# Cross-attention on one core: the ragged memory tile summed in four products, its lower-half terms laid behind the upper ones

## The chip, the core and the metric

The kernel runs on one core of a Trainium2 chip. The metric is the device time of one execution in microseconds. Five engines work side by side, each with an instruction queue of its own: TensorE (PE, products and transposes), VectorE (DVE), ScalarE (ACT), GpSimd (POOL) and SyncE (SP, which here only waits and issues transfers). They meet through semaphores, which are counters that one engine raises and another waits for. A transfer (DMA) raises its semaphore by 16 once it has landed.

## The reference, cut to what matters

Eight batches; in each, 512 rows of `x` with 512 features attend to M = 1601 rows of memory with 256 features.

```python
memory_proj = einsum('bme,de->bmd', memory, W_mem)            # (8, 1601, 512)
scores = einsum('bnd,bmd->bnm', hidden_states, memory_proj) / sqrt(512)
attn = softmax(scores, axis=-1)                                # over the 1601 memory rows
memory_context = einsum('bnm,bmd->bnd', attn, memory_proj)
gate_input = concatenate([hidden_states, memory_context], axis=-1)
gate = sigmoid(einsum('bnf,df->bnd', gate_input, W_gate) + b_gate)
fused = hidden_states + gate * memory_context
return rmsnorm(fused, norm_w)
```

Inputs and output are float32.

## The kernel before, in words

The kernel never forms `memory_proj`. It turns x into q = W_memᵀ xᵀ (256 x 512 per batch), takes scores against the raw memory, sums the memory rows with the softmax weights (u, 256 x 512), and applies W_mem to u behind that.

**Precision by halves.** Every operand of a product stands as two `float32r` tensors, an upper half (`_hi`, written by ScalarE as a rounded copy) and a lower half (`_lo`, the rest, written by VectorE as the difference of the original and the copy). A product of two such operands is three products: hi·hi, hi·lo and lo·hi.

**Tiles.** The 1601 memory rows make MT = 13 tiles of 128 partitions; the last (t = 12) has LAST = 65 rows. A batch on TensorE is, in this order: `scores` (13 tiles x 2 halves of the features x 3 products), the gate and context products of the batch before, `gate_x`, and then `weighted(b, t)` for t = 0 to 12, which sums memory rows times softmax weights over the partitions: for each of the two halves c of the memory's features L529 multiplies `mem_hi` by `p_hi`, L530 `mem_hi` by `p_lo`, L531 `mem_lo` by `p_hi`, six products of 512 columns a tile, for the last tile with 65 rows each. They add up in `bank0` (c = 0) and `bank1` (c = 1). Behind t = QUERY_AT = 9 stand the 24 products of `query`, which make the q of the next batch. Behind t = 12 the scores of the next batch follow at once.

**Softmax.** For each tile VectorE subtracts the maximum (`shift`), ScalarE takes the exponential into `p_tmp` and its rounded copy into `p_hi` (L640), and VectorE writes `p_lo` (L848, a ring of ten tiles), which raises `p_has_lo`. TensorE waits for `p_has_lo` before each tile of `weighted`. `p_hi` lies in the same memory as the scores `s`. In batch 0 ScalarE's queue has both `q_hi_part`s of the next batch ahead of the last `p_hi_part`; in the batches behind it they stand behind the loop over the tiles.

**Memory rows.** SyncE loads memory rows into `mem_raw`, two tiles a pair (L259) and the last tile's 65 rows alone (L261); ScalarE (`mem_hi_part`) and VectorE (`mem_lo_part`) split a pair into `mem_hi` and `mem_lo`. Two more sets of loads (`mem_blocks`, `x_raw`) bring memory and x in blocks of 32 for VectorE's transposes.

**SyncE's queue.** One queue issues all of these in program order, and a wait at its head holds everything behind it. An iteration of the loop is: x of the next batch (L241, 16 transfers), its memory blocks (L249), two loads of x again (L270), the rest of this batch's memory rows (L259, L261), memory blocks (L249, L252), x again, the first memory rows of the next batch (L259), and the four stores of the batch before (L275), each behind `out_done`. Batch 0 has a start of its own ahead of the loop, which ends with the loads of batch 1's first memory rows; the last batch stands behind the loop.

Of the kernel before, what the change touches and what calls it, by code (L numbers as in the profile page):

```python
# [36 lines left out]
P = 128  # L37
# [6 lines left out]
def xattn_kernel(nc: bass.Bass, x, mem, w, wg, b_gate, norm_w, out):  # L44
# [9 lines left out]
    LO_RING = 10  # L54
    RAW_PAIRS = 4
    ROW_BLOCKS = -(-M // BLOCK)
    assert N == 512 and D == 512 and C == 256 and MT % 2 == 1 and M % BLOCK == 1

    def rows(t):
# [2 lines left out]
    with ExitStack() as ctx:  # L62

        def sb(name, shape, dt=F32):
            return ctx.enter_context(nc.sbuf_tensor(name, shape, dt))

        def sem(name):
            return ctx.enter_context(nc.semaphore(name))
# [5 lines left out]
        p_tmp = sb("p_tmp", [P, TMP_RING, N])  # L74
        p_lo = sb("p_lo", [P, LO_RING, N], F32R)
        mem_raw = sb("mem_raw", [P, 2 * RAW_PAIRS, C])

        mem_blocks = sb("mem_blocks", [P, CT, ROW_BLOCKS, BLOCK])
        mem_hi = sb("mem_hi", [P, MT, C], F32R)
# [75 lines left out]

        in_x_first = [sem(f"in_x_first{k}") for k in range(NT)]
        in_mem = [sem(f"in_mem{p}") for p in range(MP)]

        in_blocks = [sem(f"in_blocks{g}") for g in range(2)]

# [73 lines left out]
        @block.sync  # L234
        def _(sp):
            def load_x(b):
                for k in range(DT):
                    for a in range(BLOCKS):
                        d = k * P + a * BLOCK
                        src = x[b, :, d : d + BLOCK].rearrange("(r j) i -> j r i", j=BLOCK)  # L240
                        sp.dma_start(x_blocks[a * BLOCK : (a + 1) * BLOCK, k, :, :], src).then_inc(in_x, 16)  # L241

            def load_mem_blocks(b, g):
                r0, r1 = ((0, 4 * P // BLOCK), (4 * P // BLOCK, ROW_BLOCKS - 1))[g]
                for c in range(CT):
                    for a in range(BLOCKS):
                        f = c * P + a * BLOCK
                        src = mem[b, r0 * BLOCK : r1 * BLOCK, f : f + BLOCK].rearrange("(r j) i -> j r i", j=BLOCK)
                        sp.dma_start(mem_blocks[a * BLOCK : (a + 1) * BLOCK, c, r0:r1, :], src).then_inc(in_blocks[g], 16)  # L249
                if g == 1:  # L250

                    sp.dma_start(mem_blocks[0:P:BLOCK, :, r1, :],  # L252
                                 mem[b, M - 1, :].rearrange("(c a i) -> a c i", c=CT, i=BLOCK)).then_inc(in_blocks[g], 16)

            def load_mem(b, p):
                slot = 2 * (p % RAW_PAIRS)
                if p < MP - 1:
                    src = mem[b, 2 * p * P : (2 * p + 2) * P, :].rearrange("(t p) c -> p t c", p=P)
                    sp.dma_start(mem_raw[:, slot : slot + 2, :], src).then_inc(in_mem[p], 16)  # L259
                else:  # L260
                    sp.dma_start(mem_raw[0:LAST, slot, :], mem[b, (MT - 1) * P : M, :]).then_inc(in_mem[p], 16)  # L261

            def load_mem_again(b, p):

                behind = p - RAW_PAIRS if p >= RAW_PAIRS else min(p + RAW_PAIRS, MP - 1) - MP
                sp.wait_ge(mem_has_lo, MP * b + behind + 1)
                load_mem(b, p)

            def load_x_again(b, j):
                sp.dma_start(x_again[:, j % 2, :], x[b, j * P : (j + 1) * P, :]).then_inc(in_x_again[j % 2], 16)  # L270

            def store(b, j):

                sp.wait_ge(out_done, NT * b + j + 1)
                sp.dma_start(out[b, j * P : (j + 1) * P, :], fused[:, j, :]).then_inc(fused_free[j], 16)  # L275

            def iteration(b, last):
                if not last:

                    sp.wait_ge(xt_done, DT * b)  # L280
                    load_x(b + 1)
                    sp.wait_ge(mt_done, MP * b)
                    load_mem_blocks(b + 1, 0)

                load_x_again(b - 1, 0)
                load_x_again(b - 1, 1)
                for p in range(RAW_PAIRS, MP):
                    load_mem_again(b, p)
                if not last:

                    sp.wait_ge(mt_done, MP * b + MP - 2)
                    load_mem_blocks(b + 1, 1)
                for j in range(2, NT):

                    sp.wait_ge(fused_done, NT * (b - 1) + j - 1)
                    load_x_again(b - 1, j)
                if not last:
                    for p in range(RAW_PAIRS):
                        load_mem_again(b + 1, p)
                for j in range(NT):  # L300
                    store(b - 1, j)


            for j in range(NT):
                sp.dma_start(x_raw[:, j, :], x[0, j * P : (j + 1) * P, :]).then_inc(in_x_first[j], 16)
            for p in range(2):
                load_mem(0, p)

            sp.wait_ge(ready_pad, 1)
            load_mem_blocks(0, 1)  # L310
            for p in range(2, RAW_PAIRS):
                load_mem(0, p)
            for i in range(DT):
                sp.dma_start(wg_raw[i], wg[i * P : (i + 1) * P, :]).then_inc(in_wg, 16)
            sp.dma_start(bias_rows[:, :], b_gate.partition_broadcast(P)).then_inc(in_rows, 16)
            sp.dma_start(norm_rows[:, :], norm_w.partition_broadcast(P)).then_inc(in_rows, 16)

            load_mem_blocks(1, 0)
            for p in range(RAW_PAIRS, MP):
                load_mem_again(0, p)  # L320

            sp.wait_ge(mt_done, MP - 2)
            load_mem_blocks(1, 1)

            sp.wait_ge(pe_wt, V[-1] + 1)
            load_x(1)
            for p in range(RAW_PAIRS):
                load_mem_again(1, p)
            with sp.Fori(1, B - 1) as b:
                iteration(b, False)  # L330
            iteration(B - 1, True)

            load_x_again(B - 1, 0)
            load_x_again(B - 1, 1)
            for j in range(2, NT):

                sp.wait_ge(fused_done, NT * (B - 1) + j - 1)
                load_x_again(B - 1, j)
            for j in range(NT):

                if 0 < j < NT - 1:
                    sp.wait_ge(tail_done, j)
                else:
                    sp.wait_ge(out_done, NT * (B - 1) + (1 if j == 0 else 2))
                sp.dma_start(out[B - 1, j * P : (j + 1) * P, :], fused[:, j, :]).then_inc(fused_free[j], 16)

            for j in range(NT):
                sp.wait_ge(fused_free[j], 16 * (B + 1))
# [3 lines left out]
        def _(pe):  # L352
# [143 lines left out]
            def gate_x(b, j, first):  # L496
# [18 lines left out]
                    (xt_hi[:, k, n], xt_lo[:, k, n], wg1t_hi[:, k, :], wg1t_lo[:, k, :]) for k in range(DT)  # L515
                ]).then_inc(pe_gx, 1)

            def weighted(b, t):

                if t % 2 == 0:  # L520

                    pe.wait_ge(mem_has_lo, MP * b + t // 2 + 1)

                pe.wait_ge(p_has_lo, MT * b + t + 1)
                r = rows(t)
                for c in range(CT):
                    cs = slice(c * P, (c + 1) * P)
                    dst = bank[U_BANK + c][:, :]
                    nc.tensor.matmul(dst, mem_hi[0:r, t, cs], p_hi[0:r, t, :], start=(t == 0), stop=False)  # L529
                    nc.tensor.matmul(dst, mem_hi[0:r, t, cs], p_lo[0:r, t % LO_RING, :], start=False, stop=False)  # L530
                    last = nc.tensor.matmul(dst, mem_lo[0:r, t, cs], p_hi[0:r, t, :], start=False, stop=(t == MT - 1))  # L531
                    if c == 0 and t == MT - 1:
                        last.then_inc(pe_u_first, 1)
                last.then_inc(pe_u, 1)
# [31 lines left out]
            def iteration(b, first, last):  # L566
# [31 lines left out]

                    pe.wait_ge(gx_done, NT * b + 2)
                for t in range(MT):  # L600
                    weighted(b, t)
                    if t == QUERY_AT and not last:

                        pe.wait_ge(xt_has_lo, DT * (b + 2))
                        pe.wait_ge(gx_done, NT * (b + 1))
                        for c in range(CT):
                            query(c, range(DT))
# [30 lines left out]
        def _(act):  # L638
            def copy(dst, src):
                return nc.scalar.activation(dst, src, ACT.Copy)  # L640
# [12 lines left out]
            def mem_hi_part(b, p, first):  # L653
                if p == 0 and not first:

                    act.wait_ge(pe_u, MT * b)

                act.wait_ge(in_mem[p], 16 * (b + 1))
                ts, raw, r = mem_pair(p)
                copy(mem_hi[0:r, ts, :], mem_raw[0:r, raw, :]).then_inc(mem_has_hi, 1)  # L660

            def copy_s(b, t):
# [537 lines left out]
```

## Time and profile before

| | |
|---|---|
| Time, three runs | 549.3, 549.71 and 549.73 us; median 549.71 |
| Time of the profiled execution | 550.2 us |
| Its span, first to last instruction | 548.4 us |
| TensorE busy | 535.8 us (98%), 2432 products and transposes |
| VectorE, ScalarE, GpSimd busy | 483.7 us (88%), 335.2 us (61%), 145.5 us (27%) |
| Granted TensorE clock, mean | 0.994 of full |
| DMA, all queues | 54.25 MB, 42% of 16 engines' span |

Busy time of TensorE counts each product from its start to a modelled end, and neighbours overlap; the distance between two starts says what a product costs in a row of them. The chain that ended last follows from the last instruction back to whatever released each step, so that its shares say which engine sets the end. A wait of an engine that is not on that chain costs nothing by itself.

### The profile page before, as it was taken

Reading aid. Unit: us, or ns where it says so; the run is one execution under the profiler, and the core shown is the slowest. Engines: PE = TensorE matmul, PEld = TensorE weight load, DVE = VectorE, ACT = ScalarE, POOL = GpSimd, SP = SyncE. Lnnn points to the kernel's source line nnn. Section 1 sums busy time; section 2 is a strip of 40 time slices with the busy share of each in tenths; the row PEclk is TensorE's granted clock in tenths of the full one; section 3 lists DMA queues with packets and bytes.
Section 4 is the critical chain, followed back from the end, with each engine's and each line's share of the span. In section 5 each row is a group of like instructions: output and inputs, shape, how many; then the busy total and the mean of one; then the engine's idle time right before and its main releaser. Section 6 shows DMA issues by size and latency. Waiting matters only on the chain.

```text
span 548.4 us, 8870 instructions
## 1 busy us (share of the span) xinstructions
PE 535.8 (98%) x2432; PEld 438.6 (80%) x2432; DVE 483.7 (88%) x759; ACT 335.2 (61%) x633; POOL 145.5 (27%) x120
## 2 busy tenths in 40 slices
PE   8999999999999999999999999999999999999993
PEld 7776888888888888888888888888888888888882
DVE  3779968899799998899888997999989999889965
ACT  4576636666476655576466764666656765657544
POOL 0005600165002540036200650025400273005600
PEclk9999999999999999999999999999999999999997
DMA  9865372611585207831278114763068411201033
GB/s 225 258 125 85 93 113 76 107 58 41 125 169 96 79 0 162 183 85 38 77 126 171 57 38 111 162 100 90 5 148 178 105 38 39 95 27 38 1 116 115
DMA packets 184337, 54.25 MB, mean 99 GB/s; under 512 B 161528, under 2 KB 174848, under 8 KB 184320
## 3 DMA queue, kind: packets, MB, share of 16 engines
q1 hardware_dynamic: 183792, 53.52, 42.2%
q10 hardware_dynamic: 528, 0.52, 0.3%
q8 instruction: 8, 0.13, 0.1%
q14 instruction: 9, 0.07, 0.0%
HBM read 45.63 MB, written 8.39 MB: 99 GB/s over the span
## 4 chain that ended last, share of the span: by engine, by line
PE 92%; SPq 3%; DMA 2%; DVE 1%; issue 1%; ACT 0%; POOLq 0%; ACTq 0%; POOL 0%; DVEq 0%
PE bank L357 21%; PE bank L359 21%; PE bank L358 21%; PE bank L529 9%; PE bank L530 9%; PE bank L531 9%; DMA fused<-in_L_xattn_W_gate_dram 2%; SPq L249 2%; PE bank L549 1%; PE bank L459 1%; PE bank L563 1%; PE bank L444 1%; PE bank L432 1%; DVE fused L1001 1%; DVE fused L994 1%
## 5 line engine op out<-in xcount | busy, mean ns | idle before, releaser
L1150 POOL TENSOR_TENSOR psum_rows<-psum_rows,p_tmp 128x512 f32<-128x512 f32 (+1 forms) x88 | 124.1, 1411 | 72.7 <-ACT p_tmp L678 71.2
L848 DVE TENSOR_TENSOR p_lo<-p_tmp,p_hi 128x512 fp32r<-128x512 f32 (+1 forms) x104 | 93.4, 899 | 5.5 <-ACT p_hi L640 5.4
L678 ACT ACTIVATE p_tmp<-s 128x512 f32<-128x512 f32 (+1 forms) x104 | 65.1, 627 | 38.2 <-DVE s L889 37.6
L1150 POOL TENSOR_TENSOR psum_rows<-p_tmp 128x512 f32<-128x512 f32 x8 | 10.8, 1353 | 276.2 <-ACT p_tmp L678 276.2
L357 PE MATMUL bank<-q_hi,mt_hi 128*128 128x512 f32 (+1 forms) x208 | 81.8, 393 | 0.0
L358 PE MATMUL bank<-q_lo,mt_hi 128*128 128x512 f32 (+1 forms) x208 | 81.2, 390 | 0.0
L359 PE MATMUL bank<-q_hi,mt_lo 128*128 128x512 f32 (+1 forms) x208 | 81.2, 390 | 0.0
L530 PE MATMUL bank<-p_lo,mem_hi 128*128 128x512 f32 (+1 forms) x208 | 81.0, 389 | 0.0
L529 PE MATMUL bank<-p_hi,mem_hi 128*128 128x512 f32 (+1 forms) x208 | 81.0, 389 | 0.0
L531 PE MATMUL bank<-p_hi,mem_lo 128*128 128x512 f32 (+1 forms) x208 | 80.9, 389 | 0.0
L640 ACT ACTIVATE s<-bank 128x512 f32<-128x512 f32 (+1 forms) x104 | 62.1, 597 | 19.5 <-PE bank L359 19.1
L889 DVE TENSOR_TENSOR s<-s,bank 128x512 f32<-128x512 f32 (+1 forms) x104 | 68.5, 672 | 0.0
L860 DVE TENSOR_TENSOR run<-run,s 128x512 f32<-128x512 f32 (+1 forms) x88 | 60.0, 681 | 8.1 <-ACT s L640 5.8
L640 ACT ACTIVATE p_hi<-p_tmp 128x512 fp32r<-128x512 f32 (+1 forms) x104 | 63.5, 617 | 0.0
L357 PE MATMUL bank<-wg1t_hi,xt_hi 128*128 128x512 f32 x128 | 50.2, 392 | 0.0
L359 PE MATMUL bank<-wg1t_hi,xt_lo 128*128 128x512 f32 x128 | 49.8, 389 | 0.0
L358 PE MATMUL bank<-wg1t_lo,xt_hi 128*128 128x512 f32 x128 | 49.8, 389 | 0.0
L848 DVE TENSOR_TENSOR mt_lo<-bank,mt_hi 128x512 fp32r<-128x512 f32 (+1 forms) x56 | 34.6, 628 | 16.6 <-ACT mt_hi L640 16.6
L640 ACT ACTIVATE mt_hi<-bank 128x512 fp32r<-128x512 f32 (+1 forms) x56 | 30.1, 550 | 28.9 <-PE bank L359 28.9
L531 PEld LDWEIGHTS bank<-p_hi,mem_lo 128*128 128x128 f32 (+1 forms) x208 | 39.0, 188 | 8.2
L359 PEld LDWEIGHTS bank<-q_hi,mt_lo 128*128 128x128 f32 (+1 forms) x208 | 38.2, 184 | 9.2
L529 PEld LDWEIGHTS bank<-p_hi,mem_hi 128*128 128x128 f32 (+1 forms) x208 | 39.0, 188 | 8.2
(92 smaller groups left out, 1024.5 us busy)
## 6 DMA issues: line engine op xcount, KB each, us to landing
mem_raw<-in_ctx_dram SPq DMA_DIRECT2D x48, 256.0 KB, 3.0
mem_blocks<-in_ctx_dram SPq DMA_DIRECT2D x64, 136.0 KB
x_again<-in_x_dram SPq DMA_DIRECT2D x32, 256.0 KB, 2.7
out_dram<-fused SPq DMA_DIRECT2D x32, 256.0 KB, 2.1
x_raw<-in_x_dram SPq DMA_DIRECT2D x112, 64.0 KB, 2.0
mem_blocks<-in_ctx_dram SPq DMA_DIRECT2D x56, 64.0 KB, 2.0
x_raw<-in_x_dram SPq DMA_DIRECT2D x4, 256.0 KB, 4.9
gate<-in_L_xattn_W_gate_dram SPq DMA_DIRECT2D x2, 512.0 KB, 5.8
```

Source lines behind the costliest of these rows:

```text
L357: nc.tensor.matmul(dst, a_hi, b_hi, start=(start and i == 0), stop=False)
L358: nc.tensor.matmul(dst, a_hi, b_lo, start=False, stop=False)
L359: last = nc.tensor.matmul(dst, a_lo, b_hi, start=False, stop=(stop and i == n - 1))
L529: nc.tensor.matmul(dst, mem_hi[0:r, t, cs], p_hi[0:r, t, :], start=(t == 0), stop=False)
L530: nc.tensor.matmul(dst, mem_hi[0:r, t, cs], p_lo[0:r, t % LO_RING, :], start=False, stop=False)
L531: last = nc.tensor.matmul(dst, mem_lo[0:r, t, cs], p_hi[0:r, t, :], start=False, stop=(t == MT - 1))
L640: return nc.scalar.activation(dst, src, ACT.Copy)
L678: nc.scalar.activation(p_tmp[0:r, t % TMP_RING, :], s[0:r, t, :], ACT.Exp, scale=float(D) ** -0.5).then_inc(exp_done, 1)
L848: return nc.vector.tensor_tensor(dst, src, hi.bitcast(F32), ALU.subtract)
L860: nc.vector.tensor_tensor(run[0:r, :], a, s[0:r, t, :], ALU.max).then_inc(run_done, 1)
L889: nc.vector.tensor_tensor(s[0:r, t, :], s[0:r, t, :], bank[MAX_BANK][0:r, :], ALU.subtract).then_inc(shifted, 1)
L1150: nc.gpsimd.tensor_tensor(psum_rows[0:r, :], a, p_tmp[0:r, t % TMP_RING, :], ALU.add).then_inc(p_added, 1)
```

## The change

For the last tile of a batch (except in the last batch, which stays as it was) the 63 free partitions behind its 65 rows are used. BEHIND is 63, REST is 2.

- `mem_raw` gets a second load for that tile: the tile's first 63 rows again, on partitions 65 to 127. `in_mem[6]` then counts 32 a batch. `mem_hi_part` copies all 128 partitions of it, so that `mem_hi` holds the 65 rows and, behind them, the first 63 again. (`r = P` in it changes nothing for the other pairs.)
- `stack_last_tile(b)` on SyncE makes four transfers inside the on-chip memory: the upper half of the last 2 memory rows to `mem_lo` behind its 65 rows (after `mem_has_lo`), and, after the last `p_has_lo` of the batch, the first 63 rows of `p_lo` to `p_hi` behind its 65 rows, the 65 rows of `p_hi` to a new tile `lo_terms`, and the last 2 rows of `p_lo` behind them. All four raise `stacked`.
- `weighted_last_tile(b)` waits for `stacked` at 64 a batch and multiplies for each c `mem_hi` by `p_hi` over 128 partitions (hi·hi of 65 rows and hi·lo of 63) and `mem_lo` by `lo_terms` over 67 partitions (lo·hi of 65 rows and hi·lo of 2): four products in place of six.
- In SyncE's queue `stack_last_tile` stands between the loads of the next batch's memory rows and the stores; for batch 0 it is the last thing ahead of the loop.

```diff
@@ -54,6 +54,8 @@
     LO_RING = 10
     RAW_PAIRS = 4
     ROW_BLOCKS = -(-M // BLOCK)
+    BEHIND = P - LAST
+    REST = LAST - BEHIND
     assert N == 512 and D == 512 and C == 256 and MT % 2 == 1 and M % BLOCK == 1
 
     def rows(t):
@@ -74,6 +76,8 @@
         p_tmp = sb("p_tmp", [P, TMP_RING, N])
         p_lo = sb("p_lo", [P, LO_RING, N], F32R)
         mem_raw = sb("mem_raw", [P, 2 * RAW_PAIRS, C])
+
+        lo_terms = sb("lo_terms", [P, N], F32R)
 
         mem_blocks = sb("mem_blocks", [P, CT, ROW_BLOCKS, BLOCK])
         mem_hi = sb("mem_hi", [P, MT, C], F32R)
@@ -156,6 +160,8 @@
         in_x_first = [sem(f"in_x_first{k}") for k in range(NT)]
         in_mem = [sem(f"in_mem{p}") for p in range(MP)]
 
+        stacked = sem("stacked")
+
         in_blocks = [sem(f"in_blocks{g}") for g in range(2)]
 
         in_x_again = [sem(f"in_x_again{i}") for i in range(2)]
@@ -259,6 +265,22 @@
                     sp.dma_start(mem_raw[:, slot : slot + 2, :], src).then_inc(in_mem[p], 16)
                 else:
                     sp.dma_start(mem_raw[0:LAST, slot, :], mem[b, (MT - 1) * P : M, :]).then_inc(in_mem[p], 16)
+                    sp.dma_start(mem_raw[LAST:P, slot, :], mem[b, (MT - 1) * P : (MT - 1) * P + BEHIND, :]
+                                 ).then_inc(in_mem[p], 16)
+
+            def stack_last_tile(b):
+                def copy(dst, src):
+                    sp.dma_start(dst.bitcast(F32), src.bitcast(F32)).then_inc(stacked, 16)
+
+                t, behind = MT - 1, slice(LAST, LAST + REST)
+
+                sp.wait_ge(mem_has_lo, MP * (b + 1))
+                copy(mem_lo[behind, t, :], mem_hi[BEHIND:LAST, t, :])
+
+                sp.wait_ge(p_has_lo, MT * (b + 1))
+                copy(p_hi[LAST:P, t, :], p_lo[0:BEHIND, t % LO_RING, :])
+                copy(lo_terms[0:LAST, :], p_hi[0:LAST, t, :])
+                copy(lo_terms[behind, :], p_lo[BEHIND:LAST, t % LO_RING, :])
 
             def load_mem_again(b, p):
 
@@ -297,6 +319,7 @@
                 if not last:
                     for p in range(RAW_PAIRS):
                         load_mem_again(b + 1, p)
+                    stack_last_tile(b)
                 for j in range(NT):
                     store(b - 1, j)
 
@@ -326,6 +349,7 @@
             load_x(1)
             for p in range(RAW_PAIRS):
                 load_mem_again(1, p)
+            stack_last_tile(0)
             with sp.Fori(1, B - 1) as b:
                 iteration(b, False)
             iteration(B - 1, True)
@@ -514,6 +538,19 @@
                 product(gx_bank(j, first)[:, :], [
                     (xt_hi[:, k, n], xt_lo[:, k, n], wg1t_hi[:, k, :], wg1t_lo[:, k, :]) for k in range(DT)
                 ]).then_inc(pe_gx, 1)
+
+            def weighted_last_tile(b):
+
+                t, k = MT - 1, LAST + REST
+                pe.wait_ge(stacked, 64 * (b + 1))
+                for c in range(CT):
+                    cs = slice(c * P, (c + 1) * P)
+                    dst = bank[U_BANK + c][:, :]
+                    nc.tensor.matmul(dst, mem_hi[:, t, cs], p_hi[:, t, :], start=False, stop=False)
+                    last = nc.tensor.matmul(dst, mem_lo[0:k, t, cs], lo_terms[0:k, :], start=False, stop=True)
+                    if c == 0:
+                        last.then_inc(pe_u_first, 1)
+                last.then_inc(pe_u, 1)
 
             def weighted(b, t):
 
@@ -598,7 +635,10 @@
 
                     pe.wait_ge(gx_done, NT * b + 2)
                 for t in range(MT):
-                    weighted(b, t)
+                    if last or t < MT - 1:
+                        weighted(b, t)
+                    else:
+                        weighted_last_tile(b)
                     if t == QUERY_AT and not last:
 
                         pe.wait_ge(xt_has_lo, DT * (b + 2))
@@ -655,8 +695,9 @@
 
                     act.wait_ge(pe_u, MT * b)
 
-                act.wait_ge(in_mem[p], 16 * (b + 1))
+                act.wait_ge(in_mem[p], (16 if p < MP - 1 else 32) * (b + 1))
                 ts, raw, r = mem_pair(p)
+                r = P
                 copy(mem_hi[0:r, ts, :], mem_raw[0:r, raw, :]).then_inc(mem_has_hi, 1)
 
             def copy_s(b, t):
```

TensorE's queue from the last product of tile t = 11 in batch 0 to the first of batch 1's scores, before:

```order
L531 MATMUL bank1<-p_hi_49,mem_lo 128x512
L529 MATMUL bank0<-p_hi_49,mem_hi 128x512 [waits p_has_lo,mem_has_lo]
L530 MATMUL bank0<-p_lo,mem_hi 128x512
L531 MATMUL bank0<-p_hi_49,mem_lo 128x512
L529 MATMUL bank1<-p_hi_49,mem_hi 128x512
L530 MATMUL bank1<-p_lo,mem_hi 128x512
L531 MATMUL bank1<-p_hi_49,mem_lo 128x512
L628 UNCONDITIONAL_BRANCH
L628 ISA
L410 ISA [waits mt_has_lo]
L357 MATMUL bank2<-q_hi,mt_hi 128x512 [waits q_has_lo]
```

and the same place in the changed kernel:

```order
L568 MATMUL bank1<-p_hi_49,mem_lo 128x512
L549 MATMUL bank0<-p_hi_49,mem_hi 128x512 [waits stacked]
L550 MATMUL bank0<-lo_terms,mem_lo 128x512
L549 MATMUL bank1<-p_hi_49,mem_hi 128x512
L550 MATMUL bank1<-lo_terms,mem_lo 128x512
L668 UNCONDITIONAL_BRANCH
L668 ISA
L434 ISA [waits mt_has_lo]
L381 MATMUL bank2<-q_hi,mt_hi 128x512 [waits q_has_lo]
```

Nothing else has moved on TensorE; two products are gone and the wait is for another semaphore. SyncE's queue ahead of the loop, from batch 1's memory rows to the first load of batch 2's x, before:

```order
L259 DMA mem_raw<-in_ctx_dram 128x2x256 [waits mem_has_lo] x4
L329 UNCONDITIONAL_BRANCH
L329 ISA
L241 ISA [waits xt_done]
L241 DMA x_raw<-in_x_dram 32x16x32
```

and in the changed kernel:

```order
L265 DMA mem_raw<-in_ctx_dram 128x2x256 [waits mem_has_lo] x4
L273 DMA mem_lo<-mem_hi 2x256 [waits mem_has_lo]
L273 DMA p_hi<-p_lo 63x512 [waits p_has_lo]
L273 DMA lo_terms<-p_hi 65x512
L273 DMA lo_terms<-p_lo 2x512
L353 UNCONDITIONAL_BRANCH
L353 ISA
L247 ISA [waits xt_done]
L247 DMA x_raw<-in_x_dram 32x16x32
```

The loads of batch 2's x now stand behind a wait for batch 0's last `p_lo`. Inside the loop the four transfers stand directly ahead of the stores.

## Rows read from the trace of the kernel before

**Rows 1.** The page: busy time by engine, and the chain that ended last.

```profile
PE 535.8 (98%) x2432; PEld 438.6 (80%) x2432; DVE 483.7 (88%) x759; ACT 335.2 (61%) x633; POOL 145.5 (27%) x120
...
PE 92%; SPq 3%; DMA 2%; DVE 1%; issue 1%; ACT 0%; POOLq 0%; ACTq 0%; POOL 0%; DVEq 0%
```

**Rows 2.** All waits of TensorE: total, times, longest, in us.

```profile
PE bank L365 <- POOL ident L1162: 1.5, 1, 1.5
PE bank L563 <- DMA fused<-in_L_xattn_W_gate_dram: 1.1, 1, 1.1
PE bank L374 <- DMA x_raw<-in_x_dram: 0.2, 1, 0.2
```

**Rows 3.** Timeline, end of batch 1: start, duration in us, engine, line, operation.

```profile
137.85 0.66 DVE L848 TENSOR_TENSOR p_lo<-p_tmp,p_hi 65x512 fp32r<-65x512 f32 x1
...
140.41 2.73 DVE L1010 SCALAR_TENSOR_TENSOR fused<-fused,r_rms,norm_rows 128x512 f32<-128x512 f32 x4
143.05 1.28 DVE L848 TENSOR_TENSOR q_lo<-bank,q_hi 128x512 fp32r<-128x512 f32 x2
...
143.13 0.39 PE L530 MATMUL bank<-p_lo,mem_hi 128*128 128x512 f32 x1
143.36 0.39 PE L531 MATMUL bank<-p_hi,mem_lo 128*128 128x512 f32 x1
143.58 0.40 PE L529 MATMUL bank<-p_hi,mem_hi 65*128 65x512 f32 x1
...
144.97 0.40 PE L357 MATMUL bank<-q_hi,mt_hi 128*128 128x512 f32 x1
```

**Rows 4.** Timeline, the same place in batch 6.

```profile
460.54 0.66 DVE L848 TENSOR_TENSOR p_lo<-p_tmp,p_hi 65x512 fp32r<-65x512 f32 x1
...
466.27 0.40 PE L529 MATMUL bank<-p_hi,mem_hi 65*128 65x512 f32 x1
```

**Rows 5.** Timeline, the same place in batch 0.

```profile
76.52 0.60 ACT L640 ACTIVATE q_hi<-bank 128x512 fp32r<-128x512 f32 x1 [2.12 <-PE bank L359]
77.01 0.62 ACT L640 ACTIVATE p_hi<-p_tmp 65x512 fp32r<-65x512 f32 x1
77.66 0.69 DVE L848 TENSOR_TENSOR p_lo<-p_tmp,p_hi 65x512 fp32r<-65x512 f32 x1 [5.44 <-ACT p_hi L640]
78.81 0.39 PE L531 MATMUL bank<-p_hi,mem_lo 128*128 128x512 f32 x1
79.04 0.40 PE L529 MATMUL bank<-p_hi,mem_hi 65*128 65x512 f32 x1
...
80.42 0.40 PE L357 MATMUL bank<-q_hi,mt_hi 128*128 128x512 f32 x1
```

**Rows 6.** Timeline of SyncE's queue: ahead of batch 1, in it, and its end.

```profile
59.54 0.47 SPq L259 DMA_DIRECT2D mem_raw<-in_ctx_dram  x1
67.10 2.90 SPq L241 DMA_DIRECT2D x_raw<-in_x_dram  x5
...
81.20 0.90 SPq L270 DMA_DIRECT2D x_again<-in_x_dram  x2
86.66 0.39 SPq L259 DMA_DIRECT2D mem_raw<-in_ctx_dram  x1
...
123.04 1.27 SPq L259 DMA_DIRECT2D mem_raw<-in_ctx_dram  x2
141.18 2.32 SPq L275 DMA_DIRECT2D out_dram<-fused  x4
144.18 7.88 SPq L241 DMA_DIRECT2D x_raw<-in_x_dram  x15
```

**Rows 7.** Single lines: x loads, memory rows, stores in the loop; issue ns, landing us.

```profile
L241 SPq DMA_DIRECT2D x_raw<-in_x_dram x112: 316/348/1205, 46.5 to 410.3; - x112
DMA to landing us min/median/max: 1.8/2.0/2.8
...
L259 SPq DMA_DIRECT2D mem_raw<-in_ctx_dram x48: 368/384/575, 2.6 to 479.4; - x48
...
DMA to landing us min/median/max: 2.6/3.0/6.1
...
L275 SPq DMA_DIRECT2D out_dram<-fused x28: 332/340/391, 141.2 to 526.9; - x28
DMA to landing us min/median/max: 2.1/2.1/2.2
```

**Rows 8.** Timeline at the start: four loads in a row; TensorE restarting behind a pause.

```profile
0.74 1.81 SPq L305 DMA_DIRECT2D x_raw<-in_x_dram  x4
...
9.29 0.47 PE L357 MATMUL bank<-xt_hi,w_hi 128*128 128x512 f32 x1
9.59 0.39 PE L358 MATMUL bank<-xt_lo,w_hi 128*128 128x512 f32 x1
9.82 0.40 PE L359 MATMUL bank<-xt_hi,w_lo 128*128 128x512 f32 x1
```

**Rows 9.** Timeline of ScalarE: the split of batch 1's pair 4.

```profile
98.88 1.14 ACT L640 ACTIVATE mem_hi<-mem_raw 128x512 fp32r<-128x512 f32 x2
```

**Rows 10.** Busy time by stretch: stretch, its length, engines, granted clock, DMA share, GB/s.

```profile
24.00:28.00 4.00, 2.85 (x15) 2.26 (x15) 3.59 (x6) 2.77 (x5) 0.00 (x0) 1.00 0.55 99
...
538.90:541.30 2.40, 0.00 (x0) 0.00 (x0) 2.25 (x5) 1.56 (x5) 0.00 (x0) 1.00 0.05 20
541.30:548.40 7.10, 0.00 (x0) 0.00 (x0) 1.59 (x3) 1.93 (x4) 1.21 (x2) 0.50 0.40 148
```

## The prediction

> **What bounds the kernel now.** I read the page first, for who is busy and who is on the chain that ended last: TensorE is busy 98% of the span, and 92% of the chain is TensorE's own work [rows 1]. Then its waits: three in the whole span, 2.8 us together, all in the first 26 us [rows 2]. From there to the last products nothing holds TensorE, so each product taken out shortens the run by its place in the row, and each moment for which TensorE is made to wait lengthens it by as much. No other engine can give that back. Third, I read the timeline where the change sits, for two things: the distance between the starts of two products, and how long before TensorE's first product of the last tile that tile's `p_lo` is ready.
>
> A full tile's products start 0.23 us apart (143.13, 143.36, 143.58) [rows 3]. The duration of 0.39 in the same rows overlaps the next product and is not the price. The six products of the 65-row tile take 144.97 - 143.58 = 1.39 us [rows 3], in batch 0 80.42 - 79.04 = 1.38 [rows 5], again 0.23 each. So 65 rows cost what 128 cost, and the two new forms, over 128 and over 67 partitions, are priced like that too.
>
> The lead differs between the batches, and that decides. In batch 1 `p_lo` ends at 137.85 + 0.66 = 138.51 and the tile's first product starts at 143.58: 5.07 us of lead [rows 3]. In batch 6 it is 466.27 - 461.20 = 5.07 [rows 4]; batches 2 to 5 lie between and repeat it within 0.05 us. In batch 0 `p_lo` ends at 77.66 + 0.69 = 78.35 and the product starts at 79.04: 0.69 us [rows 5]. The reason is in the queue order of batch 0: ScalarE must copy both halves of q first, and the second (76.52) waits for TensorE's query products; only then come `p_hi` (77.01) and `p_lo` (77.66) [rows 5].
>
> **The products taken out.** Seven batches, two products each, at 1.39 / 6 = 0.23 us: 14 x 0.232 = 3.2 us off TensorE's row. All of it counts, since TensorE does not wait around it.
>
> **What could be late next in batches 1 to 6.** The next batch's scores start 0.46 us sooner against VectorE. They need the first half of `q_lo`: the pair takes 1.28 us from 143.05, so its first half is done at about 143.7, and the product that needs it starts at 144.97 [rows 3]. The lead of 1.2 us becomes 0.8; the second half is done at 144.33 and is needed three products later, at 145.2 after the change, 0.9 us ahead. Both hold, at no cost. If that cover were gone, each batch would lose what `q_lo` is late by.
>
> **The new chain.** `p_lo` ready, SyncE wakes, issues three transfers, they land, TensorE wakes. The fourth (2 rows of `mem_hi`) is issued long before: its wait is met when the memory rows ahead of it go out (59.54 in batch 0, 123.04 in batch 1) [rows 6]. Its parts:
> - Waking SyncE: next to nothing. The first of four outputs ends near 140.41 + 2.73 / 4 = 141.1 [rows 3] and its store is issued at 141.18 [rows 6].
> - Issue: four loads in a row at the start take 1.81 us [rows 8], and one issue in the loop 0.35 (348 ns) [rows 7], so their starts are (1.81 - 0.35) / 3 = 0.49 apart, with the duration of x loads. I take 0.47; the third transfer is then issued 0.94 us after the first. Bounds 0.9 and 1.1 (the 15 x loads with register work between them start 0.54 apart [rows 6]).
> - Landing: the trace has no transfer inside the on-chip memory. Nearest are x loads (64 KB) with 1.8 at least and 2.0 in the middle, at most 2.8 behind a filled queue, and stores (256 KB) with 2.1 [rows 7]. The three carry 126, 130 and 4 KB. The last to be issued is small, and the queue is empty in batches 1 to 6 (nothing is issued from 124.31 to 141.18 [rows 6]), and in batch 0 once x loads stand behind it. I take 1.9 for it, since 4 KB is nearer to the 64 KB loads than to the stores. Bounds: 1.8 and 2.8. Nothing excludes less than 1.8, as no row has both ends on the chip; that is a rival below.
>
> Together 0.94 + 1.9 = 2.85 us, with 0.05 for the wakings 2.9 (bounds 2.7 and 4.0).
>
> In batches 1 to 6 that lies inside the lead of 5.07 with 2.2 us to spare, and even the upper bound does. Free. SyncE's own work is not late either: its three issues end near 139.9, the first store is due at 141.18 [rows 6].
>
> In batch 0 the lead is 0.69. TensorE stands still for 2.9 - 0.7 = 2.2 us, from about 79.0 to 81.25. It also restarts slowly: the first product behind a standstill is followed after 0.30 us in place of 0.23 [rows 8], and one weight load must pass first. I add 0.15 (bounds 0.05 and 0.3). Cost: 2.35 us. Nobody fills this: what stands behind on TensorE is the rest of the tile and the scores, in order, and all its later work shifts.
>
> **What is queued behind the new waits.** On SyncE in batch 0, 16 x loads that were issued from 67.10 [rows 6] now go out from about 79.8, with the memory blocks, the two loads of x again and memory pairs 4 and 5 behind them. At 0.54 us an issue, 16 + 8 + 2 make 14 us: pair 4 is issued near 94.0 in place of 86.66 [rows 6]. It lands some 3 us later [rows 7], near 97. ScalarE splits it at 98.88 [rows 9], about 100.8 with the shift of batch 0. The margin is 2 us at the least, and the x loads themselves are needed only in batch 1's softmax. The wait gives back what it takes. In batches 1 to 6 the stores behind the wait are later than it by themselves. The extra load of 63 rows is one issue of 0.5 us in a queue that waits much, and full copies over 128 partitions take the columns' time as before. Free.
>
> **The sum.** -3.2 + 2.35 = -0.9 us. The profiled execution would take 550.2 - 0.9 = 549.3, its span 547.5; the median of the runs before is 549.71, half a microsecond below that execution, and the forecast for it is 548.8. With the bounds of the chain (2.7 to 4.0) and of the restart the sum runs from -1.2 to +0.4.
>
> By the Trainium skill ("DMA: Bandwidth & Descriptors", section "Anatomy of one DMA") a transfer has a fixed part near 2.0 us and then runs at 436 GB/s; its formula is fitted to another issuing path. By it, as an estimate, the 130 KB copy would take 2.3 us and the 4 KB one 2.0, which makes the sum -0.8; it moves the forecast by 0.1.
>
> **Rivals.**
> - *Transfers inside the chip land sooner.* No DRAM is read or written. For it: the load with the least to bring has the shortest landing. Against: 64 KB and 256 KB differ by 0.1 in the middle rows, so most of a landing is the same for all. At 1.2 us of landing the standstill shrinks by 0.7, and the time is 548.1, 0.3% faster. The skill's same page ("Latency and other measured facts") holds that the access to HBM makes up most of a transfer's fixed part; by that this rival is what happens. No row before the change shows it. Chance 0.2.
> - *The chain is longer, and it ends slower.* Break-even is a standstill of 3.2 us in batch 0, a chain of 3.8. If the small copy queues behind the two large ones, its landing is near the 2.8 that loads reach behind others [rows 7]; then the sum is 0. Above 5.07 us the six other batches would pay too: at 5.3 us the time is -3.2 + 4.75 + 6 x 0.25 = +3.1, 552.8. Against: the queue is empty there. Chance of a time above 550.8: 0.05.
> - *The standstill costs clock.* At the end of the run TensorE's last product ends at 538.9 and the granted clock is full until 541.3, then 0.50, which is 1.2 in place of 2.4 GHz, after 2.4 us without work [rows 10]; it stayed full through the 1.1 us standstill near 24 us [rows 2, 10]. The new standstill has about 2.05 us without work (79.20 to 81.25), between the two. If the clock falls, each microsecond at half rate loses 0.5. The trace has no product at the lower level, so the length is open: as long as the idle that brought it (2.4 us) it costs 1.2 and the time is 550.0, within 0.2%; from 3.9 us on it is slower by over 0.2%, for example 551.0 at 4.4 us. Chance that the clock falls 0.18, that it ends above 550.8 0.06. The skill ("TensorE: Matmul & The Clock Gate", Part 1) says that the lower level is the default and that activity releases it, so that it would last into the work behind the standstill.
> - *No standstill.* If the chain hid in batch 0 too, all 3.2 us would show: 546.5. That takes a chain of 0.7 us, shorter than two issues. Chance 0.02.
>
> **How the numbers follow.** The forecast case (standstill 2.0 to 2.9 us, clock full) has 0.53, sooner landings 0.2, a longer chain 0.07 (0.05 of it above 550.8), the clock 0.18 (0.06 of it above 550.8), no standstill 0.02. About 0.2% (1.1 us) is what a measurement of this kernel can tell from no change. Faster by more needs a standstill under 2.1 us, restart included: most of the sooner landings, the fastest part of the forecast case, and no standstill, together 0.30. Slower by more is a long chain or a long fall of the clock, 0.11. The rest, 0.59, is within. The range from 547.9 to 550.2 leaves out the far ends of both.
>
> **What would show it.** Two products fewer in seven batches and scores 0.46 us sooner behind the tile in batches 1 to 6, with no wait for `stacked` there. In batch 0 one TensorE wait of 2.0 to 2.5 us, ended by a transfer to `lo_terms`, and from it on every later batch at 64.1 us from tile to tile in place of 64.54 (143.58 - 79.04) [rows 3, 5]. The row of landings for the four copies tells the sooner landings from the forecast, the granted clock behind 79 us the third rival. I am wrong if TensorE waits in batches 1 to 6, if `q_lo` becomes the last to arrive, or if batch 0's wait is under 1.5 or over 3 us.

## The result, and the profile after

The changed kernel is slower, by 0.3%. Its median is 551.83 us (22 executions, 549.06 to 554.23) against 549.83 us of the kernel before (22 executions beside them, 548.86 to 551.78); the ratio is 1.0034 with a 95% interval of 1.0023 to 1.0045. The forecast was 548.8 us, in a range from 547.9 to 550.2. The profiled execution took 552.08 us with a span of 550.3, 1.9 us more than the 548.4 of before.

The page after, busy time and the chain that ended last, beside [rows 1]:

```profile
PE 534.1 (97%) x2418; PEld 436.7 (79%) x2418; DVE 483.2 (88%) x759; ACT 334.4 (61%) x633; POOL 145.7 (26%) x120
...
PE 91%; SPq 3%; DMA 2%; DVE 1%; issue 1%; ACT 0%; POOLq 0%; ACTq 0%; POOL 0%; DVEq 0%
```

Fourteen products are gone (2432 to 2418), as the change says. TensorE is on 91% of the chain in place of 92%; something new holds it. Its waits, beside [rows 2] (total, times, longest, in us), name it:

```profile
PE bank L549 <- DMA lo_terms<-p_lo: 2.8, 1, 2.8
PE bank L389 <- POOL ident L1203: 1.5, 1, 1.5
PE bank L600 <- DMA fused<-in_L_xattn_W_gate_dram: 1.3, 1, 1.3
PE bank L398 <- DMA x_raw<-in_x_dram: 0.8, 1, 0.8
```

One wait for the stacked halves in seven batches. The timeline shows which, beside [rows 5]: batch 0, first VectorE, then SyncE's queue, then TensorE (start, duration in us, engine, line, operation).

```profile
77.94 0.69 DVE L889 TENSOR_TENSOR p_lo<-p_tmp,p_hi 65x512 fp32r<-65x512 f32 x1 [5.44 <-ACT p_hi L680]
...
78.65 0.82 SPq L273 DMA_DIRECT2D p_hi<-p_lo  x1
79.52 0.79 SPq L273 DMA_DIRECT2D lo_terms<-p_hi  x1
80.35 0.64 SPq L273 DMA_DIRECT2D lo_terms<-p_lo  x1
81.39 8.48 SPq L247 DMA_DIRECT2D x_raw<-in_x_dram  x15
...
79.08 0.39 PE L568 MATMUL bank<-p_hi,mem_lo 128*128 128x512 f32 x1
82.31 0.50 PE L549 MATMUL bank<-p_hi,mem_hi 128*128 128x512 f32 x1 [2.84 <-DMA lo_terms<-p_lo]
82.65 0.40 PE L550 MATMUL bank<-lo_terms,mem_lo 67*128 67x512 f32 x1
82.88 0.46 PE L549 MATMUL bank<-p_hi,mem_hi 128*128 128x512 f32 x1
83.14 0.63 PE L550 MATMUL bank<-lo_terms,mem_lo 67*128 67x512 f32 x1
83.57 0.63 PE L381 MATMUL bank<-q_hi,mt_hi 128*128 128x512 f32 x1
...
86.13 0.56 PE L381 MATMUL bank<-q_hi,mt_hi 128*128 128x512 f32 x1
86.53 0.39 PE L382 MATMUL bank<-q_lo,mt_hi 128*128 128x512 f32 x1
```

Two things are to be seen. The next product should have started at 79.08 + 0.23 = 79.31 and starts at 82.31: a standstill of 3.0 us. And from 83.14 on the starts lie 0.43 us apart in place of 0.23, for eight products, up to 86.53. The busy time by stretch, whose column behind POOL is the granted clock (1.00 is 2.4 GHz, 0.50 is 1.2), says why:

```profile
79.00:82.30 3.30, 0.47 (x3) 0.05 (x1) 2.02 (x4) 0.00 (x0) 0.00 (x0) 1.00 0.26 81
82.30:82.90 0.60, 0.59 (x3) 0.50 (x4) 0.00 (x0) 0.00 (x0) 0.00 (x0) 1.00 0.65 108
...
83.10:86.40 3.30, 3.30 (x9) 2.57 (x8) 2.02 (x3) 1.21 (x3) 0.00 (x0) 0.50 0.64 99
...
86.70:90.00 3.30, 3.30 (x16) 2.72 (x16) 1.50 (x3) 2.36 (x5) 0.00 (x0) 1.00 0.81 126
```

TensorE was granted 1.2 GHz in place of 2.4 for 3.4 us, and in this execution the fall came after the standstill, when it was at work again.

In batches 1 to 6 it is as forecast. Batch 1, beside [rows 3]: VectorE, SyncE, TensorE, then the same product of batch 2.

```profile
142.36 0.65 DVE L889 TENSOR_TENSOR p_lo<-p_tmp,p_hi 65x512 fp32r<-65x512 f32 x1
...
143.04 0.81 SPq L273 DMA_DIRECT2D p_hi<-p_lo  x1
143.91 0.78 SPq L273 DMA_DIRECT2D lo_terms<-p_hi  x1
144.74 0.64 SPq L273 DMA_DIRECT2D lo_terms<-p_lo  x1
...
147.86 0.39 PE L568 MATMUL bank<-p_hi,mem_lo 128*128 128x512 f32 x1
148.08 0.39 PE L549 MATMUL bank<-p_hi,mem_hi 128*128 128x512 f32 x1
...
212.18 0.39 PE L549 MATMUL bank<-p_hi,mem_hi 128*128 128x512 f32 x1
```

No gap before 148.08, and 212.18 - 148.08 = 64.10 us from batch to batch, where it was 64.54.

The sum of the profiled execution: 3.2 us saved; the standstill 3.0; the first product behind it followed after 0.34 in place of 0.23, 0.1; eight products in 86.53 - 83.14 = 3.39 us in place of 1.8, 1.6; and TensorE came to the place 0.3 us later than in the execution of before (79.08 against 78.81). That last part is the scatter of the loads at the start: the wait for the gate weights is 1.3 us here, 1.1 in the execution of before and 0.6 to 2.9 in the other traces of this document. Together +1.8, measured +1.9 in the span.

### The profile page after: what moved, and what is told of

It reads as the page before. It is cut to its first block, busy times and chain, and to the rows that moved or that the text cites. A ratio compares the mean times of both kernels' runs of the same rounds, so it can differ in the third digit from the quotient of the medians.

```text
span 550.3 us, 8895 instructions
## 1 busy us (share of the span) xinstructions
PE 534.1 (97%) x2418; PEld 436.7 (79%) x2418; DVE 483.2 (88%) x759; ACT 334.4 (61%) x633; POOL 145.7 (26%) x120
## 4 chain that ended last, share of the span: by engine, by line
PE 91%; SPq 3%; DMA 2%; DVE 1%; issue 1%; ACT 0%; POOLq 0%; ACTq 0%; POOL 0%; DVEq 0%
PE bank L381 21%; PE bank L383 21%; PE bank L382 21%; PE bank L567 8%; PE bank L568 8%; PE bank L566 8%; DMA fused<-in_L_xattn_W_gate_dram 2%; SPq L255 2%; PE bank L586 1%; PE bank L483 1%; PE bank L600 1%; PE bank L549 1%; PE bank L468 1%; PE bank L456 1%; PE bank L550 1%
## 5 line engine op out<-in xcount | busy, mean ns | idle before, releaser
L566 PE MATMUL bank<-p_hi,mem_hi 128*128 128x512 f32 (+1 forms) x194 | 75.5, 389 | 0.0
L567 PE MATMUL bank<-p_lo,mem_hi 128*128 128x512 f32 (+1 forms) x194 | 75.5, 389 | 0.0
L568 PE MATMUL bank<-p_hi,mem_lo 128*128 128x512 f32 (+1 forms) x194 | 75.5, 389 | 0.0
L382 PEld LDWEIGHTS bank<-q_lo,mt_hi 128*128 128x128 f32 (+1 forms) x208 | 38.7, 186 | 9.1
L381 PEld LDWEIGHTS bank<-q_hi,mt_hi 128*128 128x128 f32 (+1 forms) x208 | 38.7, 186 | 8.9 <-DVE q_lo L889 0.3
```

The lines of the kernel that those rows point to most:

```text
L381: nc.tensor.matmul(dst, a_hi, b_hi, start=(start and i == 0), stop=False)
L382: nc.tensor.matmul(dst, a_hi, b_lo, start=False, stop=False)
```

## The experiments

Theory A was formed from these rows: the loss is batch 0's standstill and the clock that falls behind it, and nothing else. Theory B was the rival: the transfers, the longer SyncE queue or the second load cost something in every batch. The runs of a group stood beside the kernel before on one chip: 550.38 us there in the first group (15 executions), 550.2 in the second (34).

### Batch 0 left out

```diff
-            stack_last_tile(0)
...
-                pe.wait_ge(stacked, 64 * (b + 1))
+                pe.wait_ge(stacked, 64 * b)
...
-                    if last or t < MT - 1:
+                    if first or last or t < MT - 1:
```

> Batch 0 keeps its six products and has no transfers of halves; batches 1 to 6 have the change. Theory A (all of the loss is batch 0's standstill and the clock that falls behind it): no TensorE wait for the stacked halves, clock full through 90 us, 6 x 0.46 = 2.8 us under the kernel before, near 547.0. Theory B (the transfers, the longer SyncE queue or the second load cost something in every batch): at or above the kernel before, 549.5 to 551.

Measured: 547.74 us, ratio 0.9952 (0.9939 to 0.9966), 2.6 us under the kernel before. TensorE has only its three waits at the start (1.5, 1.5 and 0.3 us). Six batches with the change bring what six batches should (2.8 us); theory B falls. Batch 0 alone turns a gain of 0.5% into a loss.

### All seven batches, the last p_hi of batch 0 ahead of q

```diff
-                        if not last and t == 12:
-                            q_hi_part(b + 1, 0)
-                            q_hi_part(b + 1, 1)
+                    if not last:
+                        q_hi_part(b + 1, 0)
+                        q_hi_part(b + 1, 1)
```

> The change in all seven batches, with ScalarE's last p_hi of batch 0 ahead of both halves of q (as the other batches have it). Theory A: p_lo of batch 0 is ready near 72 us, the lead over the tile's first product is about 7 us, the chain of 3.65 us hides, and all 14 products show: 3.2 us under the kernel before, near 546.6. If moving p_hi only delays q_hi and with it the next batch's scores: a wait for q_lo in batch 1 and less than 2.8 us. Theory B: above 549.5.

Measured: 547.47 us, ratio 0.995 (0.9937 to 0.9964), 2.9 us under the kernel before by medians; the profiled span is 545.4 us, 3.0 below the execution of before. The timeline of SyncE and of TensorE at the tile:

```profile
72.88 0.82 SPq L273 DMA_DIRECT2D p_hi<-p_lo  x1
73.75 0.79 SPq L273 DMA_DIRECT2D lo_terms<-p_hi  x1
74.58 0.64 SPq L273 DMA_DIRECT2D lo_terms<-p_lo  x1
...
78.86 0.39 PE L568 MATMUL bank<-p_hi,mem_lo 128*128 128x512 f32 x1
79.09 0.39 PE L549 MATMUL bank<-p_hi,mem_hi 128*128 128x512 f32 x1
79.32 0.40 PE L550 MATMUL bank<-lo_terms,mem_lo 67*128 67x512 f32 x1
```

The transfers leave 5.8 us sooner (72.88 against 78.65), TensorE goes from one product to the next without a gap, and it does not wait for `q_lo` either. This version beats both kernels. Between it and the one that leaves batch 0 out the runs cannot tell (0.3 us).

### The standstill filled with 13 transposes

```diff
+                if isinstance(b, int):
+                    for _ in range(13):
+                        nc.tensor.transpose(bank[7][:, 0:P], ident[:, :], ident[:, :])
                 pe.wait_ge(stacked, 64 * (b + 1))
```

> The change, with 13 transposes of the identity into a free bank on TensorE ahead of batch 0's wait (about 3.1 us of work whose result nobody reads), so that TensorE works where it stood still. Theory A: the products restart at the same time (82.3 us) or at most 0.3 later, the clock stays full, and the time is 1.6 us or more under the changed kernel, 549.7 to 550.3. If the fall of the clock has another cause than the standstill, the clock falls as before and the time stays near 551.8.

Measured: 550.88 us (11 executions, 549.08 to 554.78), ratio 1.0018 (1.0001 to 1.0035), above the 549.7 to 550.3 that theory A gave. The median can't be read for the question: 4 of the 11 took 552.8 to 554.8 us, and only one of these has a trace. In the profiled execution (554.78 us) the clock is full at the standstill, half of which the transposes fill, but it fell elsewhere: at the start TensorE waited 2.9 us for the gate weights' load (1.1 in [rows 2]), and the granted clock was low behind that.

```profile
PE bank L603 <- DMA fused<-in_L_xattn_W_gate_dram: 2.9, 1, 2.9
...
PE bank L552 <- DMA lo_terms<-p_lo: 1.5, 1, 1.5
```

```profile
24.00:28.00 4.00, 1.13 (x6) 0.94 (x6) 2.89 (x5) 1.09 (x2) 0.00 (x0) 0.78 0.70 161
28.00:32.00 4.00, 4.00 (x11) 3.12 (x11) 1.29 (x2) 1.72 (x3) 0.00 (x0) 0.50 0.55 91
```

Eleven products in four microseconds where there should be eighteen: the same loss at a place where the kernel is as before. It shows the mechanism a second time and spoils the comparison. The price of a transpose was also wrong: 13 took 1.6 us, not 3.1.

### The standstill filled with 26 transposes

> As the run with 13 transposes ahead of batch 0's wait, with 26: 13 took 1.6 us, so 26 fill the standstill of 3.0 us. Theory A (the standstill lets the clock fall): the clock stays full from 79 to 90 us, the products restart at the same time as in the changed kernel or up to 0.3 us later, and the time is 1.6 us or more below the changed kernel's. If the fall has another cause: as the changed kernel.

The edit is the one above with 26 in place of 13. Measured: 550.36 us (11 executions), ratio 1.0005 (0.9994 to 1.0016), against 552.39 for the changed kernel in the same group. The timeline and the stretches:

```profile
79.08 3.00 PE L547 MATMUL bank<-ident 128*128 128x128 f32 x26
82.15 0.50 PE L552 MATMUL bank<-p_hi,mem_hi 128*128 128x512 f32 x1
82.48 0.40 PE L553 MATMUL bank<-lo_terms,mem_lo 67*128 67x512 f32 x1
```

```profile
82.10:90.00 7.90, 7.85 (x35) 6.50 (x35) 5.17 (x9) 4.86 (x9) 0.00 (x0) 1.00 0.74 116
```

The products restart as late as in the changed kernel, at 82.15, with TensorE at work all the while; the clock stays full and 2.0 us come back. By the mean clocks that holds for 10 of the 11 executions (0.994 or more); the eleventh, 552.61 us, has 0.992. So the two causes stand apart: the standstill by itself costs what the fourteen products save, and the fall of the clock is the loss.

### The changed kernel again, and how often the clock falls

> The changed kernel again, beside the next three on one chip. Where the clock falls behind batch 0's standstill: 1.6 us or more over the kernel before; where it does not fall: within 0.3 us of it (-3.2 + 3.0 + 0.1).

Measured: 552.39 us (12 executions), ratio 1.004 (1.0019 to 1.006). Its profiled execution has a longer fall: the clock is low from 81.0 to 87.8 us. Here it fell within the standstill, 2.3 us after the last product's modelled end (78.33 + 0.39) and half a microsecond before the next one started.

```profile
78.33 0.39 PE L568 MATMUL bank<-p_hi,mem_lo 128*128 128x512 f32 x1
81.55 0.80 PE L549 MATMUL bank<-p_hi,mem_hi 128*128 128x512 f32 x1 [2.83 <-DMA lo_terms<-p_lo]
```

```profile
81.10:87.80 6.70, 6.25 (x15) 4.89 (x16) 2.02 (x3) 1.79 (x3) 0.00 (x0) 0.50 0.66 105
```

The 14 products from 81.55 to 87.69 take 6.1 us in place of 3.2, so this fall costs 2.9 us.

Each execution has its mean granted clock on record. It counts the low stretch behind the last product too, which alone makes 0.994 in the trace of before (7.1 us at half). From there a fall of 3.4 us takes off 0.003 and one of 6.8 us 0.006, as an estimate; where in the run it fell, the mean does not say. The 34 of the kernel before in this group lie at 0.993 to 0.996. Of the 34 executions of the changed kernel in both comparisons, 7 lie at 0.993 or 0.994, with a median of 549.96 us; 16 at 0.991 or 0.992, median 551.83; 11 at 0.986 to 0.989, median 553.42. Steps of 1.9 and 1.6 us, which fit no fall, a fall for 3.4 us and one for 6.8 us (two traces show the falls; the sorting of the others is inferred). The median of the first seven lies within 0.3 us of the kernel before in either comparison (549.83 and 550.2), as expected for a full clock.

### One issue less in the chain

```diff
+                sp.wait_ge(p_has_hi, MT * (b + 1))
+                copy(lo_terms[0:LAST, :], p_hi[0:LAST, t, :])
                 sp.wait_ge(p_has_lo, MT * (b + 1))
                 copy(p_hi[LAST:P, t, :], p_lo[0:BEHIND, t % LO_RING, :])
-                copy(lo_terms[0:LAST, :], p_hi[0:LAST, t, :])
```

> The copy of p_hi to lo_terms waits for p_hi alone and goes ahead of the two that wait for p_lo, in all seven batches: one issue of 0.85 us less in the chain. Theory A: it starts near 77.65 in batch 0, the first copy of p_lo near 78.5, the last one near 79.35 and lands 1.9 us later; TensorE restarts at 81.3 and has about 2.1 us without work in place of 3.0. Sum with a full clock -1.0 us against the kernel before, with the fall +0.6; whether 2.1 us let the clock fall is open, and both may occur. Batches 1 to 6: no wait.

Measured: 550.17 us (12 executions, 548.17 to 553.86), ratio 1.0004 (0.9987 to 1.0022). TensorE's wait is 2.3 us, where 2.1 was expected:

```profile
PE bank L550 <- DMA lo_terms<-p_lo: 2.3, 1, 2.3
```

```profile
79.80:82.00 2.20, 0.00 (x0) 0.00 (x0) 1.48 (x3) 0.00 (x0) 0.00 (x0) 1.00 0.40 115
82.00:86.00 4.00, 3.99 (x17) 3.31 (x18) 1.92 (x3) 1.71 (x4) 0.00 (x0) 1.00 0.65 103
```

Here the clock stayed full. By the mean clocks it did in 5 of 12 executions (0.994, median 549.58, which is 0.6 us under the kernel before where 1.0 was expected) and fell in 7 (0.988 to 0.992, 549.84 to 553.86 us). Of the 49 executions of the kernel before in the two groups and the 10 of the versions without a standstill none is under 0.993, of the 22 with transposes 3 are, so the standstill is the likely place, though no trace shows one of these seven falls. Both outcomes seem to occur at 2.3 us without work, as they do at 2.8; 7 of 12 against 27 of 34 is too few to call it less often. The changed kernel can be repaired in part this way, and a chance remains in it.

### Transfers of 64, 64 and 16 rows

```diff
-                copy(p_hi[LAST:P, t, :], p_lo[0:BEHIND, t % LO_RING, :])
-                copy(lo_terms[0:LAST, :], p_hi[0:LAST, t, :])
-                copy(lo_terms[behind, :], p_lo[BEHIND:LAST, t % LO_RING, :])
+                copy(p_hi[64:P, t, :], p_lo[0:64, t % LO_RING, :])
+                copy(lo_terms[0:64, :], p_hi[0:64, t, :])
+                copy(lo_terms[64:80, :], p_lo[49:65, t % LO_RING, :])
```

> The three late transfers with 64, 64 and 16 rows in place of 63, 65 and 2 (row 64 of p_hi is overwritten by a lower half, so this output leaves out one row's upper half). If an uneven count of rows makes the issue slow: issues of 0.35 to 0.5 us each, as loads have, and batch 0's standstill near 2.2 us. If it is that both ends lie on the chip: issues stay at 0.65 to 0.8 us and the standstill at 3.0.

Measured, in one execution: 551.72 us, TensorE's wait 2.5 us in place of 2.8, and the granted clock low from 82.6 to 86.1. The issues (ns, least, middle, most), first of this run, then of the changed kernel, and last the changed kernel's new load of 63 rows from DRAM:

```profile
L273 SPq DMA_DIRECT2D p_hi<-p_lo x7: 527/528/543, 78.6 to 463.3; - x7
L273 SPq DMA_DIRECT2D lo_terms<-p_hi x7: 582/584/589, 79.2 to 463.9; - x7
L273 SPq DMA_DIRECT2D lo_terms<-p_lo x7: 587/593/597, 79.9 to 464.5; - x7
```

```profile
L273 SPq DMA_DIRECT2D p_hi<-p_lo x7: 806/807/820, 78.7 to 463.6; - x7
L273 SPq DMA_DIRECT2D lo_terms<-p_hi x7: 781/781/786, 79.5 to 464.5; - x7
L273 SPq DMA_DIRECT2D lo_terms<-p_lo x7: 642/642/642, 80.4 to 465.3; - x7
```

```profile
L268 SPq DMA_DIRECT2D mem_raw<-in_ctx_dram x8: 296/304/315, 35.3 to 486.0; - x8
```

Neither answer alone. With even counts an issue still takes 0.53 to 0.60 us, where most loads from DRAM take 0.30 to 0.46 in the middle, among them one of 128 rows of the same 2 KB (0.36). The new counts are 0.2 to 0.28 us cheaper for the two large transfers. But the load of 63 rows takes 0.30, so an uneven count alone costs nothing. Nor does it take two ends on the chip to be slow: the kernel before has a load of 1 KB from DRAM to four partitions, and in the loop its issue takes 0.61 to 0.64 us (issue ns, least, middle, most).

```profile
L252 SPq DMA_DIRECT2D mem_blocks<-in_ctx_dram x8: 614/630/951, 12.6 to 425.8; - x8
```

What sets the price of an issue is open; no run varied the ends, the number of rows and their size one at a time.

### The kernel before, with the last p_hi ahead of q

> The kernel before with ScalarE's last p_hi of batch 0 ahead of both halves of q and nothing else: control for the run that had both. TensorE waits nowhere there, so within 0.2% of the kernel before. If the move brings a gain of its own, that gain is part of the 2.7 us measured with both.

Measured: 550.21 us, ratio 0.9994 (0.9983 to 1.0005). The new order of ScalarE brings nothing by itself; what the two edits gain together is the fourteen products.

## Why the prediction was wrong

- **What bounds the kernel, and the price of a product**: right. 14 products at 0.23 us were said to be worth 3.2 us. Batch to batch went from 64.54 to 64.10 us, and with no standstill the gain is 2.9 us (0.9937 to 0.9964 as a ratio).
- **Batches 1 to 6 free**: right, with less to spare than said. The last transfer of batch 1 is issued at 144.74 and the last count of its semaphore comes at 146.73, 1.4 us ahead of 148.08, not 2.2.
- **Batch 0 pays a standstill**: the right place, chain and reason, with the wrong size: 3.0 us in place of 2.2.
- **The step that failed first is the issue term.** The prediction took 0.47 us from one issue to the next, from loads between DRAM and the chip [rows 7, 8], and called its bounds 0.9 and 1.1 us for two. They are 79.52 - 78.65 = 0.87 and 80.35 - 79.52 = 0.83, 1.70 together. The text said that the trace had no transfer inside the on-chip memory, and widened the landing for it, but not the issue. That is 0.76 us, nearly all of what the standstill was missed by. A slow issue that the trace did have, of the 1 KB load above, is not among its rows. By itself it does not take the time out of the range: -3.2 + 3.0 + 0.1 = -0.1 us, or 549.6.
- **Landing**: right. The last transfer is issued at 80.35 and TensorE starts at 82.31, 1.96 us later with all wakings, against 1.9 + 0.05. TensorE waits for all four transfers, so this alone bounds the small one from above. The copy of 2 rows of `mem_hi`, which goes out 14 us or more ahead of the others and right behind loads, was no sooner: its last count comes 2.2 to 2.5 us after its issue (60.33 to 62.79 in batch 0). The rival of sooner landings (chance 0.2) did not happen; the sentence of the Trainium skill on which it leaned, that most of a transfer's fixed part is the access to HBM ("DMA: Bandwidth & Descriptors", "Latency and other measured facts"), is not borne out here by copies of 2 and 4 KB between two places on the chip. Each had larger transfers ahead of it; how soon such a copy lands by itself no run shows.
- **The step that took the time out of the range is the clock term**, which the sum left out. The rival was right in its mechanism and had 0.18, too little. The row of before says that 2.4 us without work were enough once [rows 10]. The forecast put its own standstill (2.05 us without work) under that and counted it as mostly safe, as if one observed fall were a threshold. With 2.8 us without work 27 of 34 executions fell, by their mean clocks, at a cost of 1.6 us in one trace and 2.9 in another. What 2.05 us would have done no run shows; with 2.3 us it was 7 of 12. The two errors are coupled, since only the longer chain made it 2.8. The range treated them one at a time, so that the sum of both (-3.2 + 3.1 + 1.6 = +1.5 and up) lay outside it.
- **Restart**: 0.15 said, 0.11 measured.
- **SyncE's delayed loads**: right. In the changed kernel x loads go out from 81.39, pair 4 at 96.07 in place of the forecast 94.0, and ScalarE splits it at 103.38; TensorE does not wait.

## What to carry to other kernels

Before a dependency is lengthened by transfers, look for the one iteration whose order differs from the loop's: here six of seven had 5 us of lead and the first had 0.7, and moving one ScalarE copy there gave 2.9 us of the 3.2. Where TensorE is the bound, a standstill like the 2.3 to 2.9 us here is not priced by its length alone, since the clock may fall with it; keep the engine at work or the standstill short. The standstills of up to 1.7 us at the start left the clock full in every trace here. And a transfer of a new kind needs its own price for the issue, not that of the nearest load.

## What the runs showed of the hardware

- SyncE needs 0.64 to 0.89 us to issue a transfer of 2 to 65 rows from one on-chip tile to another (0.89 where the 65 rows go first), 0.53 to 0.60 with 64 or 16 rows, and 0.30 to 0.46 in the middle for most loads from DRAM in the same program; but 0.61 to 0.69 for a load of 1 KB to four partitions. The copies of 2 and 4 KB, behind larger transfers, landed no sooner than loads of 64 KB do (2.0 us in the middle): the last of batch 1's counts came 1.99 us after the last issue.
- TensorE's clock can fall from 2.4 to 1.2 GHz with 2.5 to 2.9 us without work (four traces), in some executions of a program and not in others, and it fell in this program 2.4 us after the last product of all. The fall can come while the engine stands still (81.0 in one trace) or when the products have begun again (full until 83.1 in another). It lasted about 3.4 us in two traces and about 6.8 in two, and in it the products start 0.43 us apart. In one of the traces it fell 2.3 us after the last product had ended. Where the standstill was only 2.3 us, the one trace shows a full clock, and the mean clocks of 7 of 12 executions a fall somewhere. The Trainium skill ("TensorE: Matmul & The Clock Gate", Part 1) says of the start of a kernel that the number of products at the lower level varies between runs of the same kernel. No trace here has a low clock in its first products, but the falls in mid-run vary like that: by the mean clocks, 7 of 34 executions of the changed kernel had none.
- The same fall can happen at the start of this program, before anything that was changed, when the gate weights land late (2.9 us without work in one trace, 0.6 to 1.7 with a full clock in others). It is part of what scatters the times.
